# One tile in 64 of two gather stages fetched by SP, row by row, and the indices of the other gathers read in place

## What is computed

```python
x_i = x[dst]; x_j = x[src]                                  # layer 1, h = relu(layernorm(x))
h = relu(concat([x_i, x_j - x_i]) @ W1 + b1)
out = segment_max(h @ W2 + b2, dst)
...
out = concat([x[row], edge_attr])                           # layer 2, row = src, col = dst
out = relu(bn(out @ W1a + b1a)) @ W2a + b2a
out = segment_sum(out, col)
return relu(bn(concat([x, out]) @ W1b + b1b)) @ W2b + b2b
```

## Time and profile before

| what | value |
|---|---|
| median of 3 runs | 6166.33 us |
| time of the profiled execution | 6172.69 us |
| its span, first to last instruction | 6170.9 us |
| mean granted TensorE clock | 0.656 |
| stage 2 gathers, first to last | about 341 to 2895 us of the span |
| stage 4 gathers, first to last | about 3075 to 5486 us |

### The profile page before, as it was taken

The page is one execution under the profiler, slowest core; times in us unless marked ns, Lnnn a source line. Parts: engine busy times, 40 slices in busy tenths (PEclk is TensorE's granted clock), DMA queues, the critical chain, the costliest instruction groups (busy, mean ns, idle before and its releaser), DMA issues. The chain is left out here.

```text
span 6170.9 us, 34418 instructions
## 1 busy us (share of the span) xinstructions
PE 2478.8 (40%) x8675; PEld 1481.8 (24%) x8675; DVE 2036.0 (33%) x2739; ACT 1424.0 (23%) x2694; POOL 3574.8 (58%) x3776
## 2 busy tenths in 40 slices
PE   2024443333434434333033333433443333347777
PEld 1012222222222222222012121212221211125555
DVE  5212222222222222222522222222222222249995
ACT  6001111111111111111111121211111111138884
POOL 5666666665666666665666666666666666631112
PEclk9975655665665565665556666666666666668887
DMA  9412222222222222222223333333323323249993
GB/s 359 139 48 62 67 67 63 62 66 62 65 65 68 63 67 63 65 62 60 51 74 95 92 93 89 92 86 95 94 84 95 94 84 95 83 150 420 423 421 136
DMA packets 351136, 696.89 MB, mean 113 GB/s; under 512 B 133446, under 2 KB 190544, under 8 KB 304248
## 3 DMA queue, kind: packets, MB, share of 16 engines
q1 hardware_dynamic: 204908, 558.27, 24.7%
q0 software_dynamic: 119328, 128.91, 10.5%
q10 hardware_dynamic: 26706, 7.50, 0.6%
HBM read 349.70 MB, written 344.74 MB: 113 GB/s over the span
## 5 line engine op out<-in xcount | busy, mean ns | idle before, releaser
L715 POOL DMA_INDIRECT send_in<-send_table,send_idx x1664 | 1574.0, 946 | 979.5 <-issue 492.9
L1000 POOL DMA_INDIRECT pairs<-norm_table,send_idx x1664 | 1573.8, 946 | 856.2 <-issue 488.7
L727 PE MATMUL ps_msg<-hidden,w_twice 128*128 128x512 f32 x416 | 416.9, 1104 | 1530.1 <-ACT hidden L780 1069.2
L1021 PE MATMUL ps_hid<-pairs_t,w1a 128*128 128x512 f32 x832 | 623.4, 841 | 1004.6 <-issue 737.1
L1117 DVE TENSOR_SCALAR hid<-ps_hid,vec 128x512 f32<-128x512 f32 x416 | 310.5, 746 | 1814.2 <-DMA recv_edges<-hid,start_idx 1041.2
L1056 ACT COPY pairs_t<-ps_pairs 128x512 f32<-128x512 f32 x416 | 244.0, 587 | 1550.2 <-DMA recv_edges<-node_sums 1048.2
L1014 PE MATMUL ps_pairs<-ident,pairs 128*128 128x128 f32 x1664 | 352.1, 351 | 481.3 <-issue 261.4
L805 DVE TENSOR_TENSOR_SCAN filled<-mask,filled,ps_recv 128x512 f32<-128x512 f32 x208 | 266.2, 1280 | 826.2 <-issue 470.4
L1250 DVE TENSOR_TENSOR_SCAN total<-ps_mask,total,hid 128x1024 f32<-128x1024 f32 x208 | 488.7, 2350 | 50.6 <-PE ps_mask L1200 24.7
L796 DVE TENSOR_TENSOR_SCAN maxima<-mask,maxima,ps_msg 128x512 f32<-128x512 f32 x208 | 266.1, 1279 | 678.1 <-PE ps_msg L727 336.9
L727 PEld LDWEIGHTS ps_msg<-hidden,w_twice 128*128 128x128 f32 x416 | 97.5, 291 | 1591.0 <-ACT hidden L780 1109.2
(11 more groups left out here) (176 smaller groups left out, 3045.1 us busy)
## 6 DMA issues: line engine op xcount, KB each, us to landing
hid_edges<-hid SPq DMA_DIRECT2D x104, 1024.0 KB
hid<-hid_edges SPq DMA_DIRECT2D x104, 1024.0 KB
hid_edges<-rows SPq DMA_DIRECT2D x104, 1024.0 KB
recv_edges<-node_sums SPq DMA_DIRECT2D x52, 1024.0 KB
recv_in<-recv_edges SPq DMA_DIRECT2D x208, 256.0 KB
max_edges<-max_rows SPq DMA_DIRECT2D x208, 256.0 KB
edge_in<-in_edge_attr_dram SPq DMA_DIRECT2D x415, 128.0 KB
send_in<-send_table,send_idx POOLq DMA_INDIRECT x1664
```

Of the source, the lines that this page charges most:

```text
L715: pool.indirect_dma_start(out=send_in[:, s, j, t, :], out_offset=None, in_=send_table, in_offset=bass.IndirectOffsetOnAxis(ap=send_idx[:, ...
L727: nc.tensor.matmul(ps_msg[:, :], w2_twice[:, :], hidden[:, s % 2, :], start=True, stop=True).then_inc(msg_done, 1)
L1000: pool.indirect_dma_start(out=pairs[:, s, j, 0:C], out_offset=None, in_=norm_table, in_offset=bass.IndirectOffsetOnAxis(ap=send_idx[:, s / ...
L1021: nc.tensor.matmul(ps_hid[s % 2][:, :], w1a[:, :], pairs_t[:, s % 2, :], start=True, stop=True).then_inc(multiplied, 1)
```

## The change

- **Rows by SP.** In stage 2 the last tile (the last of the second block's four) of every 8th step, 25 of 1664 tiles, and in stage 4 that of every 16th step, 25 of 1664 too, is not gathered by POOL. SP fetches its 128 rows, one row per transfer (1x64, 256 bytes), into a tile of its own, `row_tile`. The indices of the tile are brought into one partition (`row_idx`), loaded into SP's registers, and each transfer takes its address from a register. SP issues 16 rows in each of 8 steps in stage 2, and 8 rows in each of 16 steps in stage 4, after the load and the store of its turn. That makes 3,200 transfers in each stage.
- **Indices in place.** The gathers that are left read their indices from `src_cols`. `send_idx`, ACT's 104 copies in each stage and POOL's waits for them are gone; POOL's wait for PE's turn stays.
- **The waits that go with it.** PE waits for the 128 rows before it turns such a tile. In stage 4 ACT copies the edge half of that tile apart (`row_edge_copied`), and SP's load and PE wait for that copy as well.

```diff
+    def issued_in(self, k):
+        m = k // self.every
+        return (m, (k % self.every) * self.per_step) if m < self.tiles else None
...
+            by_row = RowByRow(8, HB)
+            row_tile = tensor(s2, "row_tile", [P, 2, 2, C])
+            row_idx = tensor(s2, "row_idx", [1, 2, P], I32)
...
+                def send_rows(r, s):
+                    k = r * U + s
+                    if by_row.issued_in(k) is None:
+                        return
+                    m, first = by_row.issued_in(k)
+                    if first == 0:
+                        sp.wait_ge(row_idx_in, 16 * (m + 1))
+                        at_least(sp, send_turned, (m - 1) * by_row.every + 1)
+                        if m + 1 < by_row.tiles:
+                            fetch_row_idx(m + 1)
+                    _, node = nc.values_load_multi_w_load_instructions(
+                        row_idx[0:1, m % 2, first:first + by_row.per_step], engines=[mybir.EngineType.SP], min_val=0, max_val=N - 1,
+                        skip_runtime_bounds_check_because="sources are numbers of nodes")
+                    for i in range(by_row.per_step):
+                        sp.dma_start(row_tile[first + i:first + i + 1, m % 2, 1, :], send_table[bass.ds(node[i], 1), :]).then_inc(rows_in[m % 4], 16)
...
-                pipeline(sp, HB, U, [(0, load), (3, store)])
+                pipeline(sp, HB, U, [(0, load), (3, store), (0, send_rows)])
...
-                    if s % 2 == 0:
-                        at_least(pool, idx_copied, r * (U // 2) + s // 2 + 1)
                     at_least_apart(pool, send_turned, k - U + 1, pool_passed)
+                    m = by_row.of_step(k)
...
+                            if m is not None and (t, j) == (1, J - 1):
+                                continue
+                            own = m is not None and j == J - 1
+                            pool.indirect_dma_start(out=row_tile[:, m % 2, t, :] if own else send_in[:, s, j, t, :], out_offset=None, in_=send_table,
+                                                    in_offset=bass.IndirectOffsetOnAxis(ap=src_cols[:, t * HB + k, j:j + 1], axis=0)
...
+                    if m is not None:
+                        at_least(pe, rows_in[m % 4], 16 * P * (m // 4 + 1))
...
-                pipeline(act, HB, U, [(0, copy_idx), (2, copy_mask), (4, rows_out), (2, relu)])
+                pipeline(act, HB, U, [(2, copy_mask), (4, rows_out), (2, relu)])
...
+            by_row = RowByRow(16, NBLK)
...
+                    if by_row.of_step(k - U) is not None:
+                        sp.wait_ge(row_edge_copied, by_row.of_step(k - U) + 1)
...
-                pipeline(sp, NBLK, U, [(0, load), (5, store)])
+                pipeline(sp, NBLK, U, [(0, load), (5, store), (0, send_rows)])
```

More of the change, by code:

```diff
@@ L756, in _ @@
             def _(act):
[L757 to L762, removed]
                 def copy_mask(r, s):
@@ L928, in gnn_kernel @@
             sums = tensor(s4, "sums4", [P, 6])
+            by_row = RowByRow(16, NBLK)
+            row_tile = tensor(s4, "row_tile4", [P, 2, 2 * C])
+            row_idx = tensor(s4, "row_idx4", [1, 2, P], I32)
             ps_pairs = [banks(s4, f"ps_pairs{b}", [P, BLK]) for b in range(2)]
@@ L957, in _, with fetch_row_idx, send_rows @@
                 hid_v = hid_edges.rearrange("k p c -> p k c")
+                src_v = src[0:LAST_BLK * BLK].rearrange("(k p j) -> k j p", p=P, j=J)
+                def fetch_row_idx(m):
+                    with nc.allow_non_contiguous_dma(reason="indices of one tile"):
+                        sp.dma_start(row_idx[0:1, m % 2, :], src_v[(m + 1) * by_row.every, J - 1:J, :]).then_inc(row_idx_in, 16)
+                def send_rows(r, s):
+                    k = r * U + s
+                    if by_row.issued_in(k) is None:
+                        return
+                    m, first = by_row.issued_in(k)
+                    if first == 0:
+                        sp.wait_ge(row_idx_in, 16 * (m + 1))
+                        at_least(sp, turned, (m - 1) * by_row.every + 1)
+                        if m + 1 < by_row.tiles:
+                            fetch_row_idx(m + 1)
+                    _, node = nc.values_load_multi_w_load_instructions(
+                        row_idx[0:1, m % 2, first:first + by_row.per_step], engines=[mybir.EngineType.SP], min_val=0, max_val=N - 1,
+                        skip_runtime_bounds_check_because="sources are numbers of nodes")
+                    for i in range(by_row.per_step):
+                        sp.dma_start(row_tile[first + i:first + i + 1, m % 2, 0:C], norm_table[bass.ds(node[i], 1), :]).then_inc(rows_in[m % 4], 16)
+                fetch_row_idx(0)
                 sp.dma_start(w1a[:, :], W1a).then_inc(w_in, 16)
@@ L1010, in turn @@
                     at_least(pe, edge_copied, k + 1)
-                    at_least(pe, gathered[s], 16 * J * (r + 1))
+                    m = by_row.of_step(k)
+                    at_least(pe, gathered[s], 16 * (J * (r + 1) - sum(by_row.of_step(q) is not None for q in range(s, k + 1, U))))
+                    if m is not None:
+                        at_least(pe, rows_in[m % 4], 16 * P * (m // 4 + 1))
+                        at_least(pe, row_edge_copied, m + 1)
                     at_least(pe, copied, k - 1)
                     for j in range(J):
-                        mm = nc.tensor.transpose(ps_pairs[s % 2][:, j::J], pairs[:, s, j, :], ident[:, :])
+                        rows = row_tile[:, m % 2, :] if m is not None and j == J - 1 else pairs[:, s, j, :]
+                        mm = nc.tensor.transpose(ps_pairs[s % 2][:, j::J], rows, ident[:, :])
                     mm.then_inc(turned, 1)
@@ L1061, in copy_edge @@
                     at_least(act, turned, k - U + 1)
[L1062 to L1069, removed]
+                    m = by_row.of_step(k)
+                    here = J if m is None else J - 1
+                    if m is not None:
+                        nc.scalar.copy(row_tile[:, m % 2, C:2 * C], edge_in[:, s, J - 1, :]).then_inc(row_edge_copied, 1)
+                    nc.scalar.copy(pairs[:, s, 0:here, C:2 * C], edge_in[:, s, 0:here, :]).then_inc(edge_copied, 1)
                 def take_node(r, s):
```

49 lines of the change are left out of this document (28 added, 21 removed).

## The result

The changed kernel takes 7130.94 us, the median of 4 runs (7105.02 to 7142.43), beside 6163.65 us of the kernel before (4 runs, 6151.9 to 6184.61): a ratio of 1.1559, 95% interval 1.1514 to 1.1604. It is 15.6% slower, where 8% was forecast.

The account below looks back on a forecast made before the run. Each gather stage was taken as a ring of waits with no engine full, SP's longer turns then pacing the fast parts: 364 + 666 us, half given back, 515 added to 6172.7, 6,680 us as median, 8% slower; range 5,900 to 7,600.

Parts of the forecast that it names:

- SP's turn becomes the shortest step: Both gather stages: SP's turns of 11.1 and 6.0 us pace the fast parts, 1,030 us if nothing is given back; chance 0.60.
- The turn: SP's issue per step: 1.2 + 7.4 + 2.5 = 11.1 us in stage 2, 0.9 + 3.7 + 1.4 = 6.0 in stage 4.
- the forecast's own signs of being wrong: POOL's stage 2 gathers end near 2,500, PE's slow parts lengthen with POOL's bursts, or register operations are far from 0.147 us.
- SP being held up as PE is in rows 5: Rival at SP's rows: they cost more than their issue, beyond 7,600 us; 0.07, counted within the forecast's chance.
- SP's three transfers at 507.28: Stage 2, SP's queue: taking 0.32 to 0.43 us just after a slow part, they spoke against SP being held up.
- the forecast's own sum: Both stages: 364 us in stage 2 plus 666 in stage 4, 1,030 together, of which half, 515 us, was taken.
- part is given back: Both gather stages: SP makes up time while PE is in its slow part; half taken, leaving 515 us of loss.
- PE's slowness: Stage 2 from 369 us: PE falls behind while POOL is bursting; ACT copies the mask after 18.73 us of waiting.
- POOL runs through: Rival, both gather stages: POOL's stops go, 911 us at full worth, 5,255 us; half of all 5,710; chance 0.26.

Follow-up runs that it names:

- double_rows: The changed kernel with one tile in 32 fetched by SP (32 rows a step in stage 2, 16 in stage 4): 8342.83 us beside 5314.17 before, ratio 1.5701.
- few_gathers_rows: The changed kernel with POOL's gathers thinned to one tile in four after each stage's first buffers, SP's rows kept: 5116.3 us (one run).
- after_again: The changed kernel word for word, run again on an undisturbed chip: 5251.75 us beside 5311.92 us of the kernel before, ratio 0.9887.
- rows_only: The changed kernel with ACT's index copies and POOL's waits for them put back, SP's rows kept: 5258.66 us, ratio 0.9895 to the kernel before.
- in_place: The changed kernel without SP's rows, POOL gathering all tiles with indices read in place: 5314.87 us beside 5314.99 before, ratio 1.000.
- fixed_rows: The changed kernel with SP's rows from addresses known at build, without register loads or register operations: 5253.89 us, ratio 0.9884 to the kernel before.

## Why the prediction was right, and where it was not

**The direction and the bound were right.** The mechanism was that SP's turn becomes the shortest step: SP's rows lie between a store that waits for ACT and the next load, SP's wait shrank from 1311.1 to 55.1 us, its shortest step became its turn, and PE waits for `mask_in` in 199 of 208 steps. double_rows and few_gathers_rows show the same bound without any disturbance. But on the undisturbed chips the same turn of SP lies under POOL's pace and costs nothing, so as far as these runs go the forecast's direction holds only where something else already keeps POOL waiting.

**The turn was sized too high.** A row was to cost 0.46 us and the load of 16 registers 2.5. Measured: a row 0.41 us from one transfer to the next (the 0.404 of an expectation, 6.46 / 16, leaves out the first row's register operations), as its two register operations take 0.037 and 0.029 and not the 0.147 of POOL's, which was one of the forecast's own signs of being wrong; the load 1.50. The turn is 9.3 us, not 11.1, at the lower end given (9.2), and in stage 4 4.5 us, 5.8 where a store stands in it (the timeline of after_again has loads of `edge_in` at 3603.04, 3608.84, 3613.32 and 3617.80), 4.8 in the mean of four, not 6.0. The Trainium skill's page "Runtime: NRT & Kernel Launch", section on instruction fetch mechanics, has 200 ns a register even in bulk, for loads from HBM, which would be 3.2 us for 16. Here the registers are loaded from a tile in SBUF, and the trace gives 1.50 for 16 and 0.72 for 8, half of it; the measurement decides.

**The step that failed** is the one that took SP's new instructions at their own time, with only 0.07 for "SP being held up as PE is in rows 5". The argument was that SP's three transfers at 507.28 ran at their usual time. But three instructions in a pause of POOL say nothing on 51 beside a burst. In the trace of the change every second turn is held back to 21.5 us. With turns of 9.3 and 4.8 us the forecast's own sum would have been 104 x (9.3 - 7.6) = 177 us in stage 2 and 52 x (4 x 4.8 - 11.2) = 416 in stage 4, and half of the two 297 us, so 6,460 us. Measured are 634 and 290.

The second step that failed is "part is given back" in the long steps, put at half. In stage 2 they gave nothing back: they grew from 17.0 to 21.3 us, and this is two thirds of the stage's loss. So the forecast had the direction and the place of the loss, and its size came near by luck: turns taken 1.8 and 1.2 us too long made up for part of a holding back that it had given a chance of 0.07.

**What was read as PE's slowness** (18.73 us of waiting for a matmul that stood in the record long before) is by all signs the same holding back. What PE releases there comes in whole steps of 0.70 us: ACT starts at 384.38 and DVE at 395.58, 11.20 us apart, 16 x 0.70. In the signals of that trace, 48 steps of stage 2 have over 4 us between the one for the mask and the one for the turned gathers, and 42 of these spans lie within a tenth of a step of a multiple of 0.70; in after_again 35 of 146 do, little more than chance. It was seen beside POOL's bursts, and the forecast took the two for cause and effect. after_again contradicts that as a rule: POOL gathers there without a pause through both stages, and nothing is held back. What holds instructions to one in 0.70 us in the measured pair stays open. No run on the four chips shows it, and neither gathers without a pause nor the number of instructions alone brings it about there. That the recording of the instructions has a part in it is not excluded either, as every run here was recorded.

**"POOL runs through"** was worth 5,255 us at full size in the prediction. That is where the change stands on an undisturbed chip, 5,251.75 us. The agreement is chance: the kernel before takes 5,313 there, and with the index copies in place POOL hardly stops either (rows_only). So the freed index waits bring nothing (in_place, 1.000) and the gathers taken from POOL bring all of it.

**Not shown:** which part of the 15.6% comes from the rows and which from reading the indices in place, since in_place and rows_only could not be run where instructions are held back. That SP waits for nothing in that trace speaks for the rows; it is an argument, not a measurement. Nor was the share of the holding back measured by taking it away: the comparison is between places, with the same kernel.

## What to carry to other kernels

Work that is moved to an idle engine is hidden only up to the pace of the bound, and the question is how far it is from there: here SP's turn of 9.3 us lies 0.5 us under POOL's 9.85 in stage 2, the saving is worth 1.1%, and beyond POOL's pace each microsecond of SP's turn costs 208 us, one for each step. Cost it in instructions, not in transfers, and ask what happens when one in two turns takes twice as long: the margin of 5% was enough on the four chips, and none where instructions were held back. An engine that waits for half of a stage, as SP did, may have no room at all if its new work stands between a wait and a load that others need. And before a stall is put down to the work beside it, look for a trace in which the same work runs without the stall.

## What the runs showed of the hardware

- The same program (the kernel before) took 6,164 us in one place and 5,313 in another (16.0%), and four chips agreed within 0.1% on the lower value. In the first place single instructions of SP take 0.70 us, with the medians of their kind unchanged.
- A transfer of one row of 256 bytes with its address from a register costs SP 0.41 us in all: 37 ns and 29 ns of register work, 228 ns of issue, and the gaps between them. With a fixed address the two register instructions are gone, and a row takes 0.295 us (fixed_rows).
- A load of 16 registers from SBUF took 1.50 us at the median, one of 8 took 0.72.
- 225 increments of a semaphore on SP took 13.98 us, 0.062 each, with 17 ns shown as each one's duration.
